# The level from 16 to 32 of a blocked triangular inverse: 32x32 tiles instead of 64x64, and one VectorE instruction instead of two

## The reference, cut to what matters

```python
def step(S, inp):
    q_t, k_t, v_t, g_t, b_t = inp
    S = S * jnp.exp(g_t)[..., None, None]
    kv = jnp.einsum('bhk,bhkv->bhv', k_t, S)
    delta = (v_t - kv) * b_t[..., None]
    S = S + jnp.einsum('bhk,bhv->bhkv', k_t, delta)
    o = jnp.einsum('bhk,bhkv->bhv', q_t, S)
    return (S, o)
```

## Time and profile before

| | |
|---|---|
| median of three runs | 2364.73 us (2363.82 to 2368.23) |
| the profiled execution | 2356.22 us |
| its span | 2354.4 us |
| mean granted TensorE clock | 0.985 |
| PE / DVE / ACT / POOL busy | 96% / 90% / 62% / 46% |
| steps of the delta rule | 64, from 84.5 us to about 2085 us |

### The profile page before, as it was taken

How to read it: one execution, slowest core, us unless ns; L and a number is a source line. 1 busy time by engine, 2 the same in 40 slices (tenths; PEclk the granted TensorE clock), 3 DMA queues, 4 the chain that set the end, 5 groups by cost and what they waited for, 6 DMA issues and landing times. The chain is left out here.

```text
span 2354.4 us, 55470 instructions
## 1 busy us (share of the span) xinstructions
PE 2258.2 (96%) x19896; PEld 1571.7 (67%) x19896; DVE 2128.2 (90%) x4579; ACT 1458.2 (62%) x3955; POOL 1072.1 (46%) x1542
## 2 busy tenths in 40 slices
PE   5899999999999999999999999999999999888998
PEld 3576667777776767676767676776767676763554
DVE  8999999999999999999999999999999999757886
ACT  4566666666666666666676776665656655433665
POOL 3535444443435454544354444444354535214564
PEclk8999999999999999999999999999999999897999
DMA  5211122221211212222122222221111111012000
GB/s 141 62 36 50 50 56 54 56 54 52 52 48 50 55 47 65 63 61 59 47 57 57 66 63 65 63 60 40 35 33 38 23 38 23 17 56 84 24 24 27
DMA packets 289390, 120.76 MB, mean 51 GB/s; under 512 B 211510, under 2 KB 267094, under 8 KB 288604
## 3 DMA queue, kind: packets, MB, share of 16 engines
q1 hardware_dynamic: 289116, 117.21, 18.8%
HBM read 85.42 MB, written 31.74 MB: 50 GB/s over the span
## 5 line engine op out<-in xcount | busy, mean ns | idle before, releaser
L1451 DVE SCALAR_TENSOR_TENSOR d_y<-bank,d_cw,d_y 128x508 f32<-128x508 f32 (+2 forms) x576 | 422.0, 733 | 6.7 <-ACT d_y L1205 1.2
L793 POOL TENSOR_SCALAR d_ms<-d_sso 128x4 f32<-128x4 f32 x64 | 14.6, 228 | 564.1 <-ACT d_junk L1344 564.1
L777 POOL TENSOR_TENSOR d_V<-d_tok,d_kinv 128x640 f32<-128x640 f32 (+1 forms) x128 | 131.1, 1044 | 256.2 <-issue 254.0
L1629 DVE SCALAR_TENSOR_TENSOR x<-bank,x 128x512 f32<-128x512 f32 x256 | 172.1, 676 | 42.5 <-PE bank L1018 42.5
L1329 ACT ACTIVATE d_thg<-bank 128x384 f32<-128x384 f32 x128 | 62.3, 487 | 206.0 <-PE bank L973 203.7
L1205 ACT ACTIVATE d_y<-bank,d_cw 128x512 f32<-128x512 f32 x192 | 130.9, 682 | 87.2 <-PE bank L858 85.5
L1615 DVE SCALAR_TENSOR_TENSOR d_on<-d_O,d_rn,d_gate 128x192 f32<-128x192 f32 x256 | 158.5, 677 | 0.0
L823 POOL TENSOR_SCALAR d_K<-d_tok,d_Em 128x96 f32<-128x96 f32 x256 | 151.8, 611 | 0.0
L1254 ACT ACTIVATE d_tok<-bank 128x384 f32<-128x384 f32 x256 | 125.7, 491 | 36.1 <-PE bank L874 32.2
L1472 DVE SCALAR_TENSOR_TENSOR d_yv<-d_th,d_y 128x512 f32<-128x512 f32 x128 | 98.9, 772 | 52.2 <-ACT d_th L1212 44.5
L1212 ACT ACTIVATE d_th<-d_y 128x512 f32<-128x512 f32 x192 | 121.9, 635 | 38.1 <-DVE d_y L1457 25.9
(11 more groups left out here) (340 smaller groups left out, 6905.9 us busy)
## 6 DMA issues: line engine op xcount, KB each, us to landing
lt_blocks<-d_LT SPq DMA_DIRECT2D x64, 256.0 KB, 2.5
d_fw<-turned_gate_w SPq DMA_DIRECT2D x32, 256.0 KB, 3.0
d_XT<-x_blocks SPq DMA_DIRECT2D x128, 64.0 KB, 2.3
d_X<-x_blocks SPq DMA_DIRECT2D x128, 64.0 KB, 2.3
d_fw<-turned_val_w SPq DMA_DIRECT2D x32, 256.0 KB, 3.0
d_fw<-turned_out_w SPq DMA_DIRECT2D x32, 256.0 KB, 2.8
d_st<-in_L_attn_Wg_dram SPq DMA_DIRECT2D x16, 384.0 KB, 4.1
ternary<-d_ft SPq DMA_DIRECT2D x48, 128.0 KB, 2.1
```

Of the source, the lines that this page charges most:

```text
L777: last = nc.gpsimd.tensor_tensor(V[q][:, :, lo:hi], tok[q][:, :, at:at + hi - lo], over(kinv[:, :], 2, hi - lo), ALU.mult)
L1451: nc.vector.scalar_tensor_tensor(out=yy[:, :, tap:], in0=pp[:, :, 0:P - tap], scalar=cw[:, ds(st.kp, 1), t, 3 - tap], in1=yy[:, :, tap:], ...
L1629: nc.vector.scalar_tensor_tensor(out=xs, in0=bank[(4, 7, 6, 5)[i]][:, :], scalar=1.0 / (SO * SW), in1=xs, op0=ALU.mult, op1=ALU.add).then_ ...
```

## The change

The constant table gets a 64-column identity for the even blocks, a 16-column one for the odd blocks, and one mask. Y16 has 32 columns a batch (two blocks of 16) instead of 64. The matmuls of the level work on four diagonal 32x32 tiles instead of two 64x64 tiles, with 16 moving columns instead of 32. `y_16` has 16 matmuls a step instead of 8, `x_16` 28 instead of 16 (three tiles for X, four for XT). VectorE writes Y16 by one instruction of the same 128x64 form. ScalarE has three copies of 32 partitions into X instead of two of 64, and four of 32 partitions into XT instead of four of 64. The counts of semaphores that others wait for stay the same. Cut to its core:

```diff
-        "Y16": sb("Y16", [P, B, 2, 2, C_B]),
+        "Y16": sb("Y16", [P, B, 2, C_B]),
...
-            nc.gpsimd.tensor_tensor(Y16[:, :, :, :, :].rearrange("p b u w e -> p b (u w e)"), over(ident[:, 0:HB], 1, B),
-                                    over(ident[:, HB:P], 1, B), ALU.add).then_inc(s["const_ready"], 1)
+            nc.gpsimd.tensor_copy(Y16[:, :, 1, :], over(cst[:, C_IO:C_IO + C_B], 1, B)).then_inc(s["const_ready"], 1)
...
             def y_16(st):
                 hold(pe, s["X_loaded"], 64 * st.n + 64)
                 for i in range(B):
-                    for h, hf in enumerate(half):
-                        last = nc.tensor.matmul(lev[hf, i * 32:(i + 1) * 32], LT[st.p][hf, i, hf], even(X[hf, h, i, :]), start=True, stop=True)
+                    for r, q in enumerate(fourth):
+                        at = r % 2 * 32
+                        last = nc.tensor.matmul(lev[q, i * C_B:(i + 1) * C_B], LT[st.p][q, i, q], X[q, r // 2, i, at:at + C_B], start=True, stop=True)
                 last.then_inc(s["yps_done"], 1)
 
             def x_16(st):
                 hold(pe, s["Y16_ready"], st.n + 1)
                 for i in range(B):
-                    for hf in half:
-                        nc.tensor.matmul(lev[hf, P + i * 32:P + (i + 1) * 32], XT[hf, i, hf], Y16[hf, i, :, 0, :], start=True, stop=True)
-                        last = nc.tensor.matmul(lev[hf, 2 * P + i * 32:2 * P + (i + 1) * 32], Y16[hf, i, :, :, :].rearrange("p u w e -> p (u w e)"),
-                                                odd(XT[hf, i, hf]), start=True, stop=True)
+                    for q in fourth[0:3]:
+                        nc.tensor.matmul(lev[q, P + i * C_B:P + (i + 1) * C_B], XT[q, i, q], Y16[q, i, 0, :], start=True, stop=True)
+                    for r, q in enumerate(fourth):
+                        last = nc.tensor.matmul(lev[q, 2 * P + i * C_B:2 * P + (i + 1) * C_B], Y16[q, i, :, :].rearrange("p w e -> p (w e)"),
+                                                XT[q, i, r * 32 + C_B:(r + 1) * 32], start=True, stop=True)
                 last.then_inc(s["xps_done"], 1)
...
                 def copy_x32():
                     past(a, "xps_done", 2 * n + 1)
-                    for h, hf in enumerate(halves):
-                        nc.scalar.activation(X[hf, h, :, :].rearrange("p b (u w e) -> p (b u) w e", w=2, e=C_B)[:, :, 0, :],
-                                             lev[hf, P:2 * P].rearrange("p (u e) -> p u e", e=C_B), ACT.Copy).then_inc(s["X_ready"], 1)
...
+                    for r in (0, 2, 1):
+                        q, at = slice(r * 32, (r + 1) * 32), r % 2 * 32
+                        nc.scalar.activation(X[q, r // 2, :, at:at + C_B], lev[q, P:P + HB].rearrange("p (b e) -> p b e", b=B),
+                                             ACT.Copy).then_inc(s["X_ready"], 1)
+                    for r in range(4):
+                        q = slice(r * 32, (r + 1) * 32)
+                        last = nc.scalar.activation(XT[q, :, r * 32 + C_B:(r + 1) * 32], lev[q, 2 * P:2 * P + HB].rearrange("p (b e) -> p b e", b=B), ACT.Copy)
+                    last.then_inc(s["X_ready"], 1)
...
                 def y16():
                     v.wait_ge(s["yps_done"], 3 * n + 1)
-                    for u in range(2):
-                        here = slice(u * C_B, (u + 1) * C_B)
-                        last = nc.vector.scalar_tensor_tensor(out=Y16[:, :, u, 0, :], in0=bank[3][:, 0:P].rearrange("p (b e) -> p b e", b=B)[:, :, here],
-                                                              scalar=cst[:, C_MK + u:C_MK + u + 1],
-                                                              in1=cst[:, C_IE:C_IE + P].rearrange("p (b e) -> p b e", b=B)[:, :, here],
-                                                              op0=ALU.mult, op1=ALU.add)
-                    last.then_inc(s["Y16_ready"], 1)
+                    nc.vector.scalar_tensor_tensor(out=Y16[:, :, 0, :], in0=bank[3][:, 0:HB].rearrange("p (b e) -> p b e", b=B),
+                                                   scalar=cst[:, C_MK:C_MK + 1], in1=cst[:, C_IE:C_IE + HB].rearrange("p (b e) -> p b e", b=B),
+                                                   op0=ALU.mult, op1=ALU.add).then_inc(s["Y16_ready"], 1)
```

More of the change, by code:

```diff
@@ L49 @@
 C_IE = 4 * P
-C_IOTA = 5 * P
+C_B = 16
+C_IO = C_IE + P // 2
+C_IOTA = C_IO + C_B
 C_MK = C_IOTA + NSET
-C_ALL = C_MK + 3
-C_B = 16
+C_ALL = C_MK + 1
 N_BLOCK = B * P // C_B
@@ L69, in shape_constants @@
     c[:, C_NU:C_NU + P] = -1.0 * (r <= t)
-    c[:, C_IE:C_IE + P] = (r % HB) == (t // C_B % 2 * 2 * C_B + t % C_B)
-    for u in range(2):
-        c[:, C_MK + u] = (r % HB // C_B == 2 * u + 1)[:, 0]
-    c[:, C_MK + 2] = (r % HB >= HB // 2)[:, 0]
+    c[:, C_IE:C_IE + HB] = (r % (2 * C_B)) == t[:, 0:HB] % C_B
+    c[:, C_IO:C_IO + C_B] = (r % (2 * C_B)) == C_B + t[:, 0:C_B]
+    c[:, C_MK] = (r % (2 * C_B) >= C_B)[:, 0]
     e = np.arange(C_B * C_B)[None, :]
@@ L908, in _ @@
             lev = bank[3]
[L910 to L916, removed]
+            fourth = tuple(slice(r * 32, (r + 1) * 32) for r in range(4))
             def y_16(st):
@@ L1263, in decay @@
                     nc.scalar.activation(E[:, :, :].rearrange("p b t -> p (b t)"), bank[5][:, :], ACT.Exp, scale=1.0 / GS).then_inc(s["E_ready"], 1)
-                lev, halves = bank[3], (slice(0, HB), slice(HB, P))
+                lev = bank[3]
                 def copy_x32():
                     past(a, "xps_done", 2 * n + 1)
-                    for h, hf in enumerate(halves):
-                        nc.scalar.activation(X[hf, h, :, :].rearrange("p b (u w e) -> p (b u) w e", w=2, e=C_B)[:, :, 0, :],
-                                             lev[hf, P:2 * P].rearrange("p (u e) -> p u e", e=C_B), ACT.Copy).then_inc(s["X_ready"], 1)
[L1272 to L1277, removed]
+                    for r in (0, 2, 1):
[6 more added lines that the diff above has]
+                    last.then_inc(s["X_ready"], 1)
                 def copy_y32():
```

## The result

The changed kernel takes 2368.77 us (median, 2366.43 to 2379.16) beside 2364.93 us for the kernel before; the ratio is 1.0027 with a 95% interval of 1.0016 to 1.0037. Instead of the 24 us that were forecast to go, about 4 us came. The forecast value, 2340.7 us, and its range up to 2357 are both missed.

What follows compares the result with a forecast made beforehand. VectorE was taken to bound the path from `keyscale` to `gated`, PE the rest and chunk 1. A head gains 0.19 + 0.65 + 0.33 + 0.33 = 1.50 us, sixteen heads 24.0: 2364.7 - 24.0 = 2340.7 us, range 2329 to 2357.

Steps and rivals of the forecast that it cites:

- Cost of `y_16` and `x_16`: PE's matmuls on four 32x32 tiles: 0.37 and 0.63 us, saving 0.22 and 0.44, together 0.66 us a step.
- The pace of two tiles: Upper bound of PE's matmul cost: 0.017 us a pass, 88 passes 1.5 us against 1.66, next to nothing saved.
- the rival of tiles that don't overlap: Slower: PE's four diagonal tiles take 0.032 us a pass, 88 passes 2.8 us; 36 us lost, 2401 us. Chance 0.05.
- One VectorE instruction less, 0.19 us: VectorE's two writes of Y16, 0.38 us together, become one: 0.19 us less in every step bound by VectorE.
- GpSimd's place hangs on `keyscale`, which precedes `y16` and so doesn't move: GpSimd's two instructions at line 742 keep their time while VectorE's `gated` start 0.19 us earlier.
- Chunk 1, 0.65 us a step: PE-bound on both sides of `x_join`; VectorE, which waits for PE at line 1629, can follow: 0.65 us gained.
- Chunk 2, 0.33 us: Second `gated` goes free, third and fourth are held, line 1523 starts 0.33 us earlier; bounds 0 and 0.33.
- Chunk 3, 0.33 us: Same pattern as chunk 2: second `gated` free, third and fourth held, 0.33 us gained; bounds 0 and 0.33.
- Chunk 0, 0.19 us: PE waits for VectorE there, so only VectorE's saving counts: 0.19 us a step.
- ScalarE's copies, 1.25 us: Seven copies behind `x_16` take 1.25 us against 1.27, no change; 0.5 us more still hidden in chunks 1 to 3.
- The wait at `x_join`, some 40 us in all: PE's wait grows from 25 to some 40 us in all, with 0.4 to 0.8 us in chunks 2 and 3.
- PE's whole saving comes through: Rival: PE bounds chunks 1 to 3, so 16 x (0.19 + 3 x 0.66) = 34.7 us are gained, 2330. Chance 0.10.

Runs made afterwards that it cites:

- VectorE's part alone: The kernel before, 64x64 tiles kept, without the second of VectorE's two writes of Y16 (half the intermediate unwritten): 2366.57 us, ratio 1.0019.
- the run with two writes: The changed kernel, but VectorE issues the write of the intermediate twice, first into a spare tile: 2357.96 us, ratio 0.9978.
- the run with shorter copies: The changed kernel with ScalarE's seven copies reordered, X and XT of the same 32 rows behind each other: 2368.39 us, ratio 1.0020.
- the kernel with `exponents` moved: The changed kernel with GpSimd's two exponents instructions before the four K2 in chunks 1 to 3: 2337.27 us, ratio 0.9872; repeat 2330.78 us, 0.9876.
- the old tiles: The kernel before (64x64 tiles, two VectorE writes) with GpSimd's exponents before K2 in chunks 1 to 3: 2351.73 us, ratio 0.9956.

## Why the prediction was wrong, step by step

- **Cost of `y_16` and `x_16`: right.** 0.37 and 0.62 us against 0.37 and 0.63. The pace of two tiles, the upper bound, and the rival of tiles that don't overlap are out. By the floor that the Trainium skill gives (TensorE: Matmul & The Clock Gate, Back-to-back issue gap) the 32 passes of `y_16` would, by an estimate of one floor a pass, take 0.8 us; the trace doesn't agree, with 0.37.
- **One VectorE instruction less, 0.19 us: right in size**, and `gated` starts about that much earlier in chunks 1 and 2 (0.19 and 0.24).
- **"GpSimd's place hangs on `keyscale`, which precedes `y16` and so doesn't move": this is the step that failed.** Between `keyscale` and `exponents` stand the four `K2`, and the last of them collided with `gated`. A place that follows from an engine's own list is fixed only if nothing in that list is held by the engine that is being moved. The row that showed it stood in the trace of before: `K2` as a group took 2.26 us in chunk 1 and 2.05 in chunks 2 and 3, where `gated` starts later against it.
- **Chunk 1, 0.65 us a step: wrong in sign.** "With its own gain it can follow" looked at the wait for PE at line 1629 only, and not at the hold that had been used for chunks 2 and 3. It was in the trace: the fourth `gated` and line 1523 were already the held ones, and the third had started 0.36 us before `exponents` (6.43 and 6.79 from `y_16`). `exponents` came 0.23 us earlier, and the third `gated` 0.11 later, since the first two now lose 0.13 and 0.17 us beside `K2`; that closes the distance to 0.02. 15 steps gave +11.3 us instead of -9.8; this alone is 21 of the 27 us by which the sum over 60 steps misses its forecast (-22.5 to +4.3). Of the 11.3 us, 5.0 are the lower clock of three steps (last section), and 6.3 are left for the hold; VectorE's part alone, with the full clock, lost 6.4. A second thing was wrong here: the forecast read one early step and took all of chunk 1 for PE-bound, but in the late steps the fourth `gated` ends as late as anything else that `high` waits for, so TensorE's saving gives nothing there, as the run with two writes shows.
- **Chunk 2, 0.33 us: 0.23 measured, by another way.** The hold moved to the fourth `gated` alone, since here `K2` is now held (2.46 us instead of 2.05) and pushes `exponents` back. `x_join` starts 0.77 us earlier, but the step doesn't follow: PE waits at line 979 for VectorE's `add_x` (0.57 us). With TensorE and the hold both shorter, VectorE's list as a whole seems to be the bound there; no run tests that.
- **Chunk 3, 0.33 us: 0.03 in the median, next to the stated lower bound of 0.** The second `gated` starts 0.02 us ahead of `exponents` and is held as before. `gated` starts only 0.07 us earlier; the other 0.12 was lost in line 1450, which takes 0.29 us beside `K2` and took 0.17.
- **Chunk 0, 0.19 us: right in the first pair of profiles**, 0.15 a step; in the second pair stalls cover it (the medians are 29.88 and 29.89).
- **ScalarE's copies, 1.25 us: mis-sized**, 1.62. An XT copy was costed by the mean of two kinds of distance. The cover held in time, as the run with shorter copies shows, but not in full: `y_32` waits 62 times instead of 17, and with `exponents` moved this costs time in the chunk-2 steps of heads 6 to 11.
- **The wait at `x_join`, some 40 us in all: 44.8, but for another reason.** About half of it, 22 us, lies in chunk 1, which held 6 before and for which the forecast had no growth; in chunk 2, where 0.4 to 0.8 us a step were forecast, the wait fell from 0.3 to 0.2. A total that fits doesn't show that its parts do.
- **The rivals.** "PE's whole saving comes through" fits the kernel with `exponents` moved only in part: in chunk 3 it does, but the change gives 14.5 us there and not 34.7. The slower side had the wrong mechanism: it asked what TensorE's new tiles could cost, where the cost came from a VectorE instruction that was removed.

## What to carry to other kernels

Where two engines hold each other up, a shorter list on one of them is not a saving but a shift of phase: list, on both sides, which instruction is held now, how far its start is from the next one, and what the shift makes of it, in every kind of step. Then move the two out of each other's way first (here by the order of six GpSimd instructions, 0.4% on the old tiles), and only then count what the other engine saves: the same change that cost 4 us in the old order gives 14.5 in the new one.

## What the runs showed of the hardware

- **Holds between VectorE and GpSimd go both ways.** `gated` takes 0.41 us alone, 0.54 to 0.58 if `K2` holds it, and up to 1.27 if its row starts some 0.02 us before an `exponents` instruction. A `K2` takes 0.52 alone and 0.73 if `gated` holds it (0.93 in chunk 2). Even a 32x8 copy of VectorE took 1.00 us.
- **Four 32x32 tiles (diagonal ones, each with partitions of its own) run side by side on one PSUM bank:** 32 passes of 16 columns take 0.37 us, 0.012 a pass, as long as the 16 passes on two tiles in the earlier trace rows.
- **ScalarE overlaps two copies by 0.09 us only where the second begins on the same row** (0.12 against 0.21 to 0.24 us, start to start, for copies of 32 rows). The Trainium skill, ScalarE: Activation LUTs, section "What ACT_TABLE_LOAD costs", gives an overlap of about 93 ns for activations back to back; the trace agrees for the pairs of one row, and for the others not.
- **PE's clock fell behind long waits in the middle of the stage.** The kernel before shows the full clock between 120 and 2000 us in both profiles (the second has one lower stretch at 107). In the changed kernel the granted clock halves, from 2.4 to 1.2 GHz, for 3.4 us at four places in either profile, three of them in chunk-1 steps in the first and one in the second. Three profiles have the new tiles with GpSimd's old order and a full VectorE saving (the changed kernel twice, and with paired copies). In them 13 of the waits at `x_join` in chunk 1 were of 1.5 us, and 6 of these were followed by such a stretch; none of the shorter ones there was. But elsewhere in the changed kernel one came behind a wait of 1.34 us at `y_32`, another behind 1.38. A window and PE's rows around one:

```profile
1119.00:1130.00 11.00, 9.48 (x60) 6.27 (x59) 9.66 (x21) 7.21 (x17) 3.93 (x5) 0.84 0.13 37
```

```profile
1123.33 0.68 PE L953 MATMUL bank<-d_XT,d_YJ 128*64 128x64 f32 x8 [1.52 <-ACT d_YJ L1288]
...
1126.50 1.87 PE L857 MATMUL bank<-hhi,d_wa0h 128*128 128x512 f16 x4
1128.21 1.03 PE L857 MATMUL bank<-hhi,d_wa0l 128*128 128x512 f16 x4
```

Four matmuls that take 1.03 us took 1.87, and such a step 34.38 instead of 32.72 us: 3 x 1.66 = 5.0 of the 11.3 us lost in chunk 1 in the first profile. In the VectorE-alone run PE waits there for 1.06 us, the clock stays up, and chunk 1 still loses 6.4 us. Why only some of the waits are followed by it stays open.
